# Eight transformer layers on one core: order of loads, fills and layout steps at four stage starts

## What is computed

```python
x = x + L0_attn(_layernorm(x), ...)   # 16 heads of 8 features, full softmax over 2048 tokens
x = x + L0_ffn(_layernorm(x), ...)
x = x + L1_attn(_layernorm(x), ...)   # 16 heads of 64 features, full softmax over 2048 tokens
x = x + L1_ffn(_layernorm(x), ...)    # gated
x = x + L2_attn(_layernorm(x), ...)   # each token sees its two neighbours
x = x + L2_ffn(_layernorm(x), ...)    # best of 8 experts
x = x + L3_attn(_layernorm(x), ...)   # recurrent memory in chunks of 64 tokens
x = x + L3_ffn(_layernorm(x), ...)    # best two of 8 experts, and a shared one
```

## Time and profile before

| | us |
|---|---|
| median of three runs | 3012.32 (3011.58 to 3017.68) |
| profiled execution | 3017.96 |
| its span, first to last instruction | 3016.2 |

### The profile page before, as it was taken

How to read it: one execution, slowest core, us unless ns; L and a number is a source line. 1 busy time by engine, 2 the same in 40 slices (tenths; PEclk the granted TensorE clock), 3 DMA queues, 4 the chain that set the end, 5 groups by cost and what they waited for, 6 DMA issues and landing times. The chain is left out here.

```text
span 3016.2 us, 43117 instructions
## 1 busy us (share of the span) xinstructions
PE 2854.5 (95%) x15612; PEld 1776.5 (59%) x15612; DVE 2171.2 (72%) x4488; ACT 1481.5 (49%) x2925; POOL 744.3 (25%) x614
## 2 busy tenths in 40 slices
PE   6999999999976999999999999999999978889798
PEld 3666666666644555555555555555555445456587
DVE  7888888888835877777777778777777366666655
ACT  3666666666651344444444444444444432444443
POOL 1000000000000244444344444444444410056200
PEclk7999999999997899999999999999999988855599
DMA  4121212121005011111011111011110010000000
GB/s 101 28 50 31 51 30 53 28 53 23 1 11 127 1 42 43 43 28 36 22 43 42 43 31 41 15 42 43 43 43 1 1 41 8 8 1 2 18 1 15
DMA packets 45619, 96.57 MB, mean 32 GB/s; under 512 B 13456, under 2 KB 33632, under 8 KB 37216
## 3 DMA queue, kind: packets, MB, share of 16 engines
q1 hardware_dynamic: 45408, 93.83, 13.7%
HBM read 35.87 MB, written 7.34 MB: 14 GB/s over the span
## 5 line engine op out<-in xcount | busy, mean ns | idle before, releaser
L1014 ACT ACTIVATE l1a_PT<-l1a_st 128x512 f32<-128x512 f32 x1024 | 596.6, 598 | 760.8 <-PE l1a_st L930 757.2
L1031 DVE TENSOR_REDUCE l1a_m<-l1a_aux 128x1 f32<-128x512 f32 x1024 | 667.9, 688 | 126.3 <-PE l1a_aux L892 124.4
L981 POOL TENSOR_TENSOR l1a_acc<-l1a_acc,l1a_PT 128x1024 f32<-128x1024 f32 x224 | 569.7, 2543 | 680.3 <-ACT l1a_PT L1014 680.3
L507 DVE TENSOR_REDUCE l0s_mquad<-l0s_mx 128x1 f32<-128x512 f32 x1024 | 635.5, 684 | 140.6 <-PE l0s_mx L387 140.6
L481 ACT ACTIVATE l0s_PT<-l0s_st 128x512 f32<-128x512 f32 x1024 | 528.9, 602 | 272.9 <-PE l0s_st L403 270.4
L943 PE MATMUL l1a_ov<-l1a_PT,l1a_V 128*64 128x512 f32 x2048 | 495.7, 605 | 0.0
L928 PE MATMUL l1a_st<-l1a_QA,l1a_KA 128*128 128x512 f32 x1024 | 447.4, 437 | 2.3 <-issue 2.3
L403 PE MATMUL l0s_st<-l_QS,l_KS 128*128 128x512 f32 x1024 | 437.9, 431 | 5.0 <-ACT l0s_PT L481 2.9
L387 PE MATMUL l0s_mx<-l_KS,l_QS 120*128 120x512 f32 x1024 | 417.0, 415 | 7.1 <-DMA l_QS<-qk_rows 7.0
L930 PE MATMUL l1a_st<-l1a_QB,l1a_KB 65*128 65x512 f32 x1024 | 406.1, 397 | 0.0
L892 PE MATMUL l1a_aux<-l1a_KA,l1a_QA 128*128 128x512 f32 x1024 | 398.5, 436 | 1.3 <-DVE l1a_lo L1043 0.8
(11 more groups left out here) (391 smaller groups left out, 2647.0 us busy)
## 6 DMA issues: line engine op xcount, KB each, us to landing
l1a_KA<-l1a_hi SPq DMA_DIRECT2D x32, 512.0 KB, 8.1
l_KS<-qk_rows SPq DMA_DIRECT2D x64, 192.0 KB
l_QS<-qk_rows SPq DMA_DIRECT2D x128, 96.0 KB
l1a_QA<-l1a_hi SPq DMA_DIRECT2D x16, 512.0 KB, 4.6
l1a_QA<-l1a_lo SPq DMA_DIRECT2D x16, 512.0 KB, 8.9
l1a_QB<-l1a_hi SPq DMA_DIRECT2D x16, 512.0 KB, 4.6
l1a_KB<-l1a_lo SPq DMA_DIRECT2D x16, 512.0 KB, 6.5
qk_rows<-l0s_hi SPq DMA_DIRECT2D x64, 64.0 KB, 5.0
```

Of the source, the lines that this page charges most:

```text
L507: nc.vector.tensor_reduce(mquad[:, u % 2, tile, g:g + 1], mx[:, n % MX0, :], axis=AX.X, op=ALU.max).then_inc(mx_free[n % MX0], 1)
L981: nc.gpsimd.tensor_tensor(acc[:, h % 2, 1, :], first, PT[:, g % PT_SLOTS, :], ALU.add).then_inc(added_pool, 1)
L1014: nc.scalar.activation(PT[:, g % PT_SLOTS, (u % 2) * CW:(u % 2 + 1) * CW], st[:, u % ST1, :], ACT.Exp, scale=1.0 / float(np.sqrt(HD1))).th ...
L1031: nc.vector.tensor_reduce(m4[:, b, q, c:c + 1], src, axis=AX.X, op=ALU.max).then_inc(aux_read, 1)
```

## The change

1. First attention: GpSimd waits, through a new function `scaled_all`, for all normalized tiles before it fills V.
2. Second attention: the weights of heads 0 and 1 and the bias get a load and a semaphore of their own (`w0_in`), the rest follows (`w_in`). The first head's QA and KA are laid out by ScalarE (two copies per chunk) and VectorE (two copies per chunk); only its QB and KB still go by transfers. In the list `before`, the second head's projections stand behind 20 of the first head's 64 maxima. TensorE waits for the row of ones only ahead of the loop.
3. Fourth attention: the chunk pattern is loaded first, with a semaphore of its own, and GpSimd's copy waits for it alone. `rate` stands behind the last convolution, and its products are 128 columns wide (each next one writes over all but the first column). `turn` stands ahead of the last `gate`. ScalarE makes its moves, the end values and the table load ahead of the last `convolved`. VectorE sums the squares last.
4. Last feed-forward: the down weights `w2` are loaded last, with a semaphore of their own, waited for ahead of the down products. The shared bias is added chunk by chunk behind the first four multiplications.

```diff
+    def scaled_all(self, engine):
+        engine.wait_ge(self.s["normed"], (self.r + 1) * (NT - NC))
+        engine.wait_ge(self.s["scaled"], (self.r + 1) * NC)
...
         def _(pool):
+            norm.scaled_all(pool)
             nc.gpsimd.memset(V[:, :, :, :], 0.0).then_inc(v_set, 1)
...
-            sp.dma_start(Wqk[:, :, :], W["L1_attn_Wqk"]).then_inc(w_in, 16)
-            sp.dma_start(bias[:, :], W["L1_attn_bqk"]).then_inc(w_in, 16)
+            sp.dma_start(Wqk[:, 0:2, :], W["L1_attn_Wqk"][:, 0:2, :]).then_inc(w0_in, 16)
+            sp.dma_start(bias[:, :], W["L1_attn_bqk"]).then_inc(w0_in, 16)
+            sp.dma_start(Wqk[:, 2:H1, :], W["L1_attn_Wqk"][:, 2:H1, :]).then_inc(w_in, 16)
...
-        before = ([("qk", 0, c) for c in range(NC)] + [("v", 0, c) for c in range(NC)] + [("qk", 1, c) for c in range(NC)]
-                  + [("max", 0, i) for i in range(NT * NC)] + [("mt", 0, 0)])
+        before = ([("qk", 0, c) for c in range(NC)] + [("v", 0, c) for c in range(NC)]
+                  + [("max", 0, i) for i in range(5 * NC)] + [("qk", 1, c) for c in range(NC)]
+                  + [("max", 0, i) for i in range(5 * NC, NT * NC)] + [("mt", 0, 0)])
...
-                for h in range(2):
-                    place_a(h)
-                    place_b(h)
+                sp.wait_ge(hi_done, NC)
+                sp.wait_ge(aux_read, read(("qk", 0, NC - 1)))
+                place_b(0)
+                place_a(1)
+                place_b(1)
...
-                pe.wait_ge(w_in, 64)
-                pe.wait_ge(ones_set, 1)
+                pe.wait_ge(w0_in, 32)
                 for key in plan[0]:
                     aux_task(key)
                 pe.wait_ge(small_in, 48)
+                pe.wait_ge(ones_set, 1)
...
-                for h in range(2):
-                    for i in range(NC):
-                        round_hi(h, i)
+                for i in range(NC):
+                    round_hi(0, i)
+                    at = slice(i * CW, (i + 1) * CW)
+                    act.wait_ge(hi_done, i + 1)
+                    for rows, tile in ((slice(0, HD1), QA), (slice(HD1, 2 * HD1), KA)):
+                        nc.scalar.activation(tile[rows, 0, at], hi[rows, at].bitcast(F32), ACT.Copy).then_inc(placed_a[0], 4)
+                for i in range(NC):
+                    round_hi(1, i)
...
+                        if h == 0:
+                            dve.wait_ge(aux_read, slot[key] + 1)
+                            for tile, part, rows in ((QA, lo, slice(0, HD1)), (KA, hi, slice(HD1, 2 * HD1))):
+                                other = slice(HD1, 2 * HD1) if tile is QA else slice(0, HD1)
+                                nc.vector.tensor_copy(tile[other, 0, at], part[rows, at].bitcast(F32)).then_inc(placed_a[0], 4)
...
+            sp.dma_start(w2[:, :, :, :], W["L3_ffn_w2"]).then_inc(w2_in, 16)
...
+                        pe.wait_ge(w2_in, 16)
                         for d in downs_of[g - 1]:
...
-                add_bias(nc, X, sb2, shared_bias)
...
                     multiply(u)
+                    if u < NC:
+                        x = X[:, TPC * u:TPC * (u + 1), :]
+                        nc.vector.tensor_tensor(x, x, sb2[:, :].unsqueeze(1).broadcast_to([P, TPC, D]), ALU.add
+                                                ).then_inc(shared_bias, 1)
...
+        sp.dma_start(delta[:, :], W["chunk_delta"]).then_inc(delta_in, 16)
         sp.dma_start(wp[:, :, :], W["L3_attn_proj"]).then_inc(loaded.sem, 16)
...
-                    last = nc.tensor.matmul(pp[:, 1, n:n + 1], soft[MAIN, n * P:(n + 1) * P], lead[MAIN, 1:2],
-                                            start=True, stop=True)
+                    last = nc.tensor.matmul(pp[:, 1, n:n + P], soft[MAIN, n * P:(n + 1) * P],
+                                            lead[MAIN, 1:2].broadcast_to([CHUNK, P]), start=True, stop=True)
...
             gate(1)
+            convolve(3)
             rate()
-            convolve(3)
             key_query(1)
             gate(2)
             key_query(2)
+            turn()
             gate(3)
-            turn()
             key_query(3)
...
             move(1)
+            move(2)
+            move(3)
+            nc.scalar.activation(T["Eend"][:, :], chunks(T["E"][MAIN, :])[:, :, CHUNK - 1], ACT.Copy)
+            nc.scalar.activation(gate_half[:, :], cw[:, 0:1], ACT.Tanh)
             convolved(3)
...
-            pool.wait_ge(loaded.sem, loaded.all)
+            pool.wait_ge(delta_in, 16)
...
+            key_query(3)
             dve.wait_ge(ksq_done, 2)
             nc.vector.tensor_reduce(T["k2"][:, :], ksq[:, :, :], axis=AX.X, op=ALU.add)
-            key_query(3)
```

More of the change, by code:

```diff
@@ L898, in aux_task @@
                     elif kind == "v":
+                        if h == 0 and i == 0:
+                            pe.wait_ge(w_in, 48)
                         for j in range(TPC):
@@ L1746, in l3_ffn @@
         expert_no = sb("expert_no", [P, E8])
-        loaded = W["loads"].stage(7)
+        loaded = W["loads"].stage(6)
+        w2_in = sem("w2_in")
         def load(sp):
```

17 lines of the change are left out of this document (7 added, 10 removed).

## The result

The changed kernel takes **2988.07 us** (2987.95 to 2989.69, three runs) where the kernel before takes 3012.32. The medians are 24.3 us apart; the ratio of the runs is 0.9906 with a 95% interval of 0.9892 to 0.9920, which is 24 to 33 us. In the three later comparisons the kernel before took 3016.02 to 3018.20 us, so 24.3 lies at the low end. The forecast was 2986 us with a range of 2979 to 2999. The profiled execution of the changed kernel has a span of 2987.9 us against 3016.2, 28.3 us less, where the sum of the prediction has 26.1.

What follows compares the result with a forecast made beforehand. TensorE, busy without a gap in the second attention's unchanged loop, left only its waits to win: 6.5 + 13.0 + 1.6 + 4.5 + 0.5 = 26.1 us, giving 2991.9 from the profiled execution, 2986 us at the median, range 2979 to 2999.

Steps and rivals of the forecast that it cites:

- The fill behind the normalization: First attention: normalizing steps no longer shut out by GpSimd's fill of V; 6.5 us won, bounds 4.8 and 6.6.
- The choice between 4.8 and the full value: First attention: does the moved fill shut out VectorE's first subtraction? Forecast no, 6.5 us; rival yes, total 2988, chance 0.10.
- The second attention, 13.0: Start of the second attention: engines lay out the first head's factors, so its maxima end 13.0 us sooner.
- the hole: Second attention: gap in VectorE's maxima while the second head's projections run; 7.3 us at 1.2 GHz, 3.9 at 2.4 GHz.
- The rival of 2.4 GHz: Second attention: projections among the maxima run at 2.4 GHz; 29.5 us won in all, 2983 us; chance 0.09.
- The copy of the chunk pattern, 1.6: Fourth attention's preparation: GpSimd's copy moves away from the normalizing steps; 1.6 us won, bounds 0 and 1.7.
- The new order, 4.5: Fourth attention's preparation: last convolution ahead of wide rate products, sum of squares last; 4.5 us won, bounds 0.5 and 5.3.
- The rival that the clock falls under the wide products: Fourth attention's preparation: granted clock falls under the wide rate products too; 22.1 us won in all, 2990 us; chance 0.11.
- The last feed-forward, 0.5: Last feed-forward: 1.0 us from the earlier start, less 0.5 for the bias additions; 0.5 us won, bounds -0.7 and 1.2.
- GpSimd's first low part releases the first product: Last feed-forward: TensorE's start is released by GpSimd's low part instead of the loads' landing, 1.0 us sooner.
- The loop's period: Second attention's head loop: handover of a head's maxima every 89.6 us was forecast to stay unchanged.
- The rival that ends on the slow side: Second attention's loop settles into another order of additions and ScalarE waits for GpSimd: 32 us per 0.13, 3018 us; chance 0.03.

Runs made afterwards that it cites:

- the second comparison: The changed kernel run once more beside the kernel before on the same chip: 2989.73 us against 3016.02, ratio 0.9913, faster by 26.2 us.
- e11_fill_pieces: The kernel before with GpSimd's fill of V cut into eight fills at their old place: 3015.10 us against 3018.20, ratio 0.9992.
- e1_fill: The kernel before plus only the first attention's change, GpSimd's fills of V waiting for all normalized tiles: 3010.47 us against 3017.33, ratio 0.9973.
- e3_prep: The kernel before plus only the fourth attention's preparation change: 3011.08 us against 3017.33, ratio 0.9975.
- e8_keep_clock: The changed kernel with an unread 128-column product behind each of the first head's maxima in both attentions: 2989.09 us, ratio 0.9910 to the kernel before.

## Why the prediction was right, point by point

The total was right to 2 us both ways: 26.1 forecast, 24.3 in the medians, 26.2 in the second comparison, 28.3 in the two traces. Part of that is luck. By the stretches the parts add up to 27 to 31 us; two of the three runs of the kernel before in the first comparison were quick ones, and the terms for the second attention and the preparation were too low by 3.0 and 2.4 us, that for the last feed-forward too high by 0.7.

- **The fill behind the normalization, 6.5: right.** Every kernel with it starts its first transposition 6.4 us sooner. The choice between 4.8 and the full value was right too, the subtraction isn't shut out. What the prediction hadn't seen is that this stage varies by 2 us from one execution to the next through the clock's first rise, and that its two bounds were narrower than that.
- **The second attention, 13.0: mechanism right, size 3 us too low.** The maxima started at 937.1, 18.0 us behind the first transposition; the forecast had 17.1 to 18.1. Twenty maxima took 12.0 us and 44 took 26.4, as forecast. The term that was mis-sized is the hole: 7.3 us forecast at half clock, 5.2 measured. The prediction read the clock 19 to 29 us behind the start of the 64 maxima and applied it 12 us behind it, where it was another: the maxima begin at 1.00, it falls only at 946.4, and in the hole it is back at 1.00 after two microseconds. The rival of 2.4 GHz with its 3.9 us was half right. Another 0.9 us are in the loop, whose first steps run at half clock for 3.6 us instead of 6.0; the prediction had no term for it. VectorE's share of a chunk was added up to 1.65 us where 0.76 and twice 0.41 are 1.58; ScalarE paces the chunks, at 2.09 us each where 2.0 were forecast, so nothing hangs on it.
- **The copy of the chunk pattern, 1.6: right for the normalizing steps, not as a certainty, and not the whole.** 1.9 to 2.0 us up to the first convolution where the loads land as in the trace of before, nothing where they land 0.3 us later. The lower bound of 0 was the other case, for a different reason than the one given. Behind the first convolution go another 1.6 us with it, by the clock; the prediction had no term for them.
- **The new order, 4.5: 6.5 measured against before, 4.9 against old code whose copy is out of the way.** The convolution took the 3.6 us of the forecast. The rate products took 3.83 instead of 4.6: the prediction sized them from a block of eight in 1.16 us, 0.145 each, and theirs are 0.12 apart. The blocks took 1.07 each, not 1.1, and the half-clock blocks behind the turning block, for which 0.8 of the possible 1.6 us had been set aside, didn't come. The rival that the clock falls under the wide products did not come true in this order, but it does in the old one behind a late copy; the prediction weighed the columns alone and not what stands ahead of them.
- **The last feed-forward, 0.5: wrong in sign.** The step that failed is "GpSimd's first low part releases the first product". With the large load at the end the remaining six still landed 2 us behind ScalarE's first high part, so the start moved 0.3 us only (7.4 to 7.1 behind the transposition), and the whole stage came out no shorter. That the four bias additions among the multiplications took the 0.3 us back is likely, but no run has them apart.
- **The loop's period** stayed: 1249.2 us from second to last row, where the old code gives 1248.7 to 1249.5. The rival that ends on the slow side had no part in it.

## What to carry to other kernels

A step of VectorE that takes turns with GpSimd pays the whole length of a long GpSimd instruction beside it, here 6.9 us: move the long fill to where VectorE does something that it doesn't delay, here a subtraction with two inputs, or cut it up, which gave back 2.6 us of 6.5. Where TensorE is paced by another engine, ask what its clock does in the work behind; a few products that nobody reads, in the paced stretch and in the wait at its end, were worth 5 us here, and those in the paced stretch without the others next to nothing. Size an edit by the stretch between two instructions over several executions of unchanged code before believing a microsecond from one trace.

## What was unexpected of the hardware

- The granted clock's column says nothing before its first change: sixteen identical products took 7.03 to 8.26 us in thirteen kernels and 8.53 in e11_fill_pieces, the first few in part at half speed, all at a shown 1.00. Behind the old code they took 7.03 to 8.26, behind the new 7.03 to 8.17, so their length doesn't go by the code in front.
- Such spread is not in one place alone. From the first attention's output to the second attention's first transposition, where nothing is changed, four kernels took 54.0 to 54.5 us and ten 56.1 to 56.7; e1_fill is among the four, e3_prep among the ten.
- TensorE busy for 10.0 of 10 us with matmuls at half clock, each paced by VectorE's 0.60 us, didn't get the full clock back (windows of after from 960 to 970, granted clock 0.50). One product of 128 columns more behind each did it in the first attention of e8_keep_clock (0.50 from 36 to 38, 0.67 over 38 to 44, 1.00 from 44 on).
- In e8_keep_clock the granted clock fell from 1.00 to 0.50 at 980.7. The last product of the maxima had ended at 978.55; since then TensorE had been idle for 1.49 us and had begun one product of 0.28 us at 980.04.
- From the scan's first product to the last feed-forward's first transposition nothing is changed, and yet it takes 194.7 to 195.0 us in the six kernels with the old second attention and 195.3 to 195.6 in the eight with the new one. It is steady and 0.6 us large; its cause stays open.
